# Decoder layer on one core: residual loads and row stores of the attentions move from the sync engine's queue to GpSimd's

## The reference

```
x = layernorm(x + causal_attention(x))            # 16 heads of 32, low-rank parts added to q, k, v, o weights
h = ln(x + attention(x, x)) ; h = ln(h + attention(h, ctx)) ; h = ln(h + relu(h @ fc1) @ fc2)
x = layernorm(x + h)
x = layernorm(x + bitlinear(gelu(bitlinear(x))))  # rows rounded to 8 bits, weights to -1, 0, 1
```

## Time and profile before

| | |
|---|---|
| median of 3 runs | 3247.62 us (3247.37 to 3250.29) |
| the profiled execution | 3245.53 us, span 3243.7 us |
| busy: PE, DVE, ACT, POOL | 2988.8, 2567.3, 1995.7, 1349.9 us |
| data moved by DMA | 405.86 MB, mean 125 GB/s |
| of it issued by SP (and a little by ACT) | 348.64 MB, 41.0% of the engines' time |
| issued by POOL | 51.40 MB, 5.1% |

### The profile page before, as it was taken

The page is one execution under the profiler, slowest core; times in us unless marked ns, Lnnn a source line. Parts: engine busy times, 40 slices in busy tenths (PEclk is TensorE's granted clock), DMA queues, the critical chain, the costliest instruction groups (busy, mean ns, idle before and its releaser), DMA issues.

```text
span 3243.7 us, 87025 instructions
## 1 busy us (share of the span) xinstructions
PE 2988.8 (92%) x34642; PEld 2369.2 (73%) x34642; DVE 2567.3 (79%) x4750; ACT 1995.7 (62%) x4650; POOL 1349.9 (42%) x1273
## 2 busy tenths in 40 slices
PE   7998999988999769999999999999889999999996
PEld 4987888888899647777877778877765565565662
DVE  4776888888899669999999999999846666666666
ACT  2655565667787537777777777877655445344352
POOL 0675632257765544444344344443132232222232
PEclk9999999999999889999999999999899999999997
DMA  4666655456554546655655555554341121211212
GB/s 127 185 206 223 194 180 153 135 159 202 174 162 140 150 118 134 141 141 125 140 137 134 137 135 147 134 129 106 125 152 40 46 53 53 56 45 44 56 40 49
DMA packets 430834, 405.86 MB, mean 125 GB/s; under 512 B 272368, under 2 KB 346240, under 8 KB 429280
## 3 DMA queue, kind: packets, MB, share of 16 engines
q1 hardware_dynamic: 415600, 348.64, 41.0%
q0 software_dynamic: 14576, 51.40, 5.1%
q10 hardware_dynamic: 256, 0.26, 0.0%
HBM read 239.98 MB, written 109.52 MB: 108 GB/s over the span
## 4 chain that ended last, share of the span: by engine, by line
PE 51%; DVE 18%; DMA 13%; ACT 8%; issue 4%; SPq 4%; POOL 1%; ACTq 0%; DVEq 0%; POOLq 0%
PE at_ps L769 22%; PE at_ps L1430 4%; PE at_ps L911 4%; PE at_ps L855 4%; DVE at_mx_cross L988 4%; DVE at_p L997 3%; DMA self_spill<-at_proj 3%; PE at_ps L1444 3%; PE at_ps L890 3%; PE at_ps L1455 3%; PE at_ps L1411 2%; ACT at_ps L945 2%; DVE at_proj L981 2%; DMA at_o_raw<-at_values 2%; PE at_ps L865 2%
## 5 line engine op out<-in xcount | busy, mean ns | idle before, releaser
L944 ACT ACTIVATE at_p<-at_ps 125x448 f16<-125x448 f32 (+2 forms) x1280 | 676.9, 529 | 285.9 <-PE at_ps L890 196.5
L997 DVE TENSOR_TENSOR at_p<-at_ps,at_p 125x448 f16<-125x448 f32 (+2 forms) x1280 | 750.5, 596 | 129.3 <-ACT at_ps L945 119.3
L945 ACT ACTIVATE at_ps<-at_ps 125x448 f32<-125x448 f32 (+2 forms) x1280 | 679.5, 531 | 0.0
L988 DVE TENSOR_REDUCE at_mx_cross<-at_ps 128x1 f32<-128x750 f32 x512 | 476.7, 931 | 26.9 <-PE at_ps L855 24.5
L1070 POOL TENSOR_TENSOR at_o_sum<-at_o_raw 128x256 f32<-128x256 f32 x192 | 121.2, 631 | 782.6 <-ACT at_o_raw L951 782.1
L911 PE MATMUL at_ps<-at_values,at_p 112*128 112x65 f16 (+3 forms) x6656 | 303.3, 185 | 23.4 <-DVE at_p L997 10.5
L1478 ACT ACTIVATE at_masks<-at_ps,at_b_cols 128x256 f32<-128x256 f32 x224 | 106.7, 476 | 336.2 <-PE at_ps L1411 336.1
L992 DVE TENSOR_REDUCE at_mx<-at_ps 112x2 f32<-112x448 f32 (+1 forms) x512 | 303.9, 609 | 10.0 <-PE at_ps L865 7.0
L1411 PE MATMUL at_ps<-at_xt,at_early 128*128 128x256 f16 x1792 | 302.1, 276 | 8.9 <-ACT at_w_first L1479 6.1
L911 PEld LDWEIGHTS at_ps<-at_values,at_p 112*128 112x128 f16 (+1 forms) x6656 | 267.2, 97 | 49.3 <-ACT at_o_raw L951 19.7
L1430 PE MATMUL at_ps<-at_w_second,at_w_first 128*128 128x512 f16 x896 | 283.6, 379 | 0.0
(11 more groups left out here) (217 smaller groups left out, 6941.7 us busy)
## 6 DMA issues: line engine op xcount, KB each, us to landing
at_x_res<-x SPq DMA_DIRECT2D x124, 256.0 KB, 3.2
cross_spill<-at_proj SPq DMA_DIRECT2D x64, 487.0 KB, 3.2
at_x_rows<-x SPq DMA_DIRECT2D x92, 256.0 KB, 3.1
at_prep<-bit POOLq DMA_DIRECT2D x32, 512.0 KB, 5.5
at_early<-ctx SPq DMA_DIRECT2D x32, 512.0 KB, 5.3
at_stacks<-cross_spill SPq DMA_DIRECT2D x64, 243.5 KB, 3.7
causal_spill<-at_proj SPq DMA_DIRECT2D x64, 224.0 KB, 3.5
at_stacks<-causal_spill SPq DMA_DIRECT2D x128, 112.0 KB, 2.3
```

The source lines that it names most:

```text
L944: act.activation(mem.p_hi[0:self.KC, n % 4, 0:self.P_COLS], scores, ACT.Exp, scale=EXP_SCALE)
L945: act.activation(scores, scores, ACT.Exp, scale=EXP_SCALE).then_inc(self.exp_done, 1)
L988: dve.tensor_reduce(self.mx[:, at, t, h:h + 1], mem.ps_qk[:, :, 0:self.KT // 2], AX.XY, ALU.max).then_inc(self.max_done, 1)
L997: dve.tensor_tensor(mem.p_lo[0:self.KC, n % 4, cols], mem.ps_st[0:self.KC, self.st_bank(b, g, n), cols], mem.p_hi[0:self.KC, n % 4, cols], ...
```

## The change

Events of kind `residual` and `store` do nothing on SP any more. POOL handles them, with the same semaphores, the same transfers, and at the same place of the list. In the feed-forward stage the first writing of `at_y` waits in addition until all stores of cross have landed.

```diff
--- before.py
+++ after.py
@@ -703,15 +703,6 @@
             to = mem.ct[b % 2].rearrange("p i c k -> p (i c) k")
             sp.dma_start(to[:, :, c * P:c * P + n_rows], mem.c_parts[0:n_rows, c].rearrange("p i d -> p (i d)"),
                          transpose=True).then_inc(self.ct_in[b % 2], 16)
-        elif kind == "residual":
-            if before is not None:
-                sp.wait_ge(self.stored, 32 * (b - self.NB + 1))
-            if b >= 2 and self.back(b, 2).has_wo:
-                sp.wait_ge(self.proj_free, self.free_index["y1", b - 2, 0] + 1)
-            elif b >= 2:
-                sp.wait_ge(self.z_done, b - 2 - self.NB + 1)
-            for t, q0 in enumerate(TILES):
-                sp.dma_start(mem.x_res[:, b % 2, t, :], self.x_in[b - self.b0, q0:q0 + P, :]).then_inc(self.x_res_in[b % 2], 16)
         elif kind == "spill":
             sp.wait_ge(self.proj_free, self.all_projected(b, g))
             wait(sp, self.stacked[g % 2], self.stack_count(b, g, 0))
@@ -729,13 +720,6 @@
         elif kind == "row":
             sp.wait_ge(*self.released(kind, b, g))
             sp.dma_start(self.qs(b, g)[96:97], self.mrow[:, g % 2, :]).then_inc(self.mrow_in[g % 2], 16)
-        elif kind == "store":
-            if self.norm is None:
-                sp.wait_ge(self.yn_done, 2 * b + 2)
-            else:
-                sp.wait_ge(self.y_done, b - self.NB + 1)
-            sp.dma_start(self.x_out[b - self.b0, 0:P, :], mem.y[:, 0, :]).then_inc(self.stored, 16)
-            sp.dma_start(self.x_out[b - self.b0, P:T, :], mem.y[2 * P - T:P, 1, :]).then_inc(self.stored, 16)
         elif kind == "weights in":
 
             for n in range(2):
@@ -1040,7 +1024,23 @@
 
     def gpsimd(self, pool, kind, b, g, n):
         mem, at = self.mem, b - self.b0
-        if kind == "split x":
+        if kind == "residual":
+            if self.before is not None:
+                pool.wait_ge(self.stored, 32 * (b - self.NB + 1))
+            if b >= 2 and self.back(b, 2).has_wo:
+                pool.wait_ge(self.proj_free, self.free_index["y1", b - 2, 0] + 1)
+            elif b >= 2:
+                pool.wait_ge(self.z_done, b - 2 - self.NB + 1)
+            for t, q0 in enumerate(TILES):
+                pool.dma_start(mem.x_res[:, b % 2, t, :], self.x_in[b - self.b0, q0:q0 + P, :]).then_inc(self.x_res_in[b % 2], 16)
+        elif kind == "store":
+            if self.norm is None:
+                pool.wait_ge(self.yn_done, 2 * b + 2)
+            else:
+                pool.wait_ge(self.y_done, b - self.NB + 1)
+            pool.dma_start(self.x_out[b - self.b0, 0:P, :], mem.y[:, 0, :]).then_inc(self.stored, 16)
+            pool.dma_start(self.x_out[b - self.b0, P:T, :], mem.y[2 * P - T:P, 1, :]).then_inc(self.stored, 16)
+        elif kind == "split x":
             pool.wait_ge(self.x_rows_in[b % 2], 32 * (b // 2 + 1))
             if at >= 1:
                 pool.wait_ge(self.xt_in[(b - 1) % 2], 32 * ((at - 1) // 2 + 1))
@@ -1618,6 +1618,8 @@
             self.row_stats(dve, self.z2, 2, self.y_dve, self.begun("y_dve", kind, b, tiles[0], 0), tiles)
         elif kind == "apply6":
             dve.wait_ge(self.y_pool, self.done("y_pool", "last", b, tiles[0]))
+            if b == 0:
+                dve.wait_ge(self.cross.stored, 32 * self.cross.b_end)
             wait(dve, self.stored, 32 * b)
             self.normalize(dve, self.y, self.z2, 2, tiles).then_inc(self.y_dve, 1)
```

## The result

The changed kernel took 3271.56 us in the median (3266.7 to 3277.53, 4 runs), the kernel before 3247.49 (3241.56 to 3250.29, 4 runs): ratio 1.0085, 95% interval 1.0068 to 1.0102. The change costs 24 us; 3232 was forecast. The profiled execution of the changed kernel took 3277.53 us, the highest of its four.

The account below looks back on a forecast made before the run. No engine was the whole bound: PE held half the span, a seventh hung on DMAs and the sync queue. Waits of 19.1 us times 0.8, plus 0.9 + 0.9, less 1.5, gave 15.6 us: 3232 us, range 3219 to 3249.

Parts of the forecast that it names:

- the seven waits behind a residual: Own layer: PE's stack waits after spills delayed by residual loads would all go, 9.7 us (bounds 4.9 to 9.7).
- eight waits behind store and load: Own layer: PE's stack waits after spills following stores and loads, 10.5 us in all; 4.5 us of gain taken.
- A wait costs its length: Own layer: a batch holding a 1.31 us wait and a short one took 28.0 us, one without waits 27.2.
- The stores: Moving them frees the sync queue: 4.5 us in own, 0.9 at the layer change, 0.9 ending cross, 1.0 lost in causal.
- The causal layer: Of its 5.5 us of PE waits for stacks, 2.0 would go, as the residual leaves between spill and stacks.
- POOL's price: Issuing on POOL takes 1.6 + 1.2 = 2.8 us a batch; delayed z costs DVE 1.5 us in all (0 to 16).
- The landings: Stores and residuals issued from POOL's queue would land in 3 to 4 us.
- The third rival: POOL's issues take twice as long, so z comes late and DVE loses 31 us: 3260 us, chance 0.13.
- The warning in the Trainium skill: Some DVE instructions lock the port through which GpSimd's DMA descriptors are written; SP or ACT advised; the rows showed no delay.
- The first rival: Shared 16 DMA engines set the landings, so spills stay late and only issue time is won: 5.8 us, 3242, chance 0.20.

Follow-up runs that it names:

- e2: The kernel before with only the stores moved to GpSimd, residual loads left on the sync engine: 3239.78 us, ratio 0.9958 to 0.9991.
- e4: The kernel before plus two small unread GpSimd loads at each place where the changed kernel issues a residual or store: 3243.07 us, ratio 0.9971 to 1.0008.
- e9: The changed kernel with residual loads cut to an eighth of their bytes from each layer's third batch on: 3243.85 us, ratio 0.9962 to 1.0004.
- e5: The kernel before, all on the sync engine, residual moved behind the stack loads in causal and own layers: 3246.53 us, ratio 0.9975 to 1.0022.
- e8: The kernel before with stores on GpSimd and, in the own layer, the sync engine's residual behind the stack loads: 3231.86 us, ratio 0.9937 to 0.9968.
- e1: The kernel before with only the residual loads moved to GpSimd, stores left on the sync engine: 3262.21 us, ratio 1.0030 to 1.0067.
- e11: The kernel before with residual loads on the scalar engine's queue and stores on GpSimd's: 3257.83 us, ratio 1.0001 to 1.0056.

## Why the prediction was wrong

**The step that failed** is the one on the seven waits behind a residual: "so that its data is through, or nearly, when the spill starts". I set the residual's new moment (901.8 + 1.2 us) against the *next* spill at 906.61 only. But the earlier trace rows already held the unit before: a spill at 898.59 that lands after 5.2 us, so with stack loads at about 904. At 903.0 the residual is a microsecond ahead of them. That step was booked at -9.7 us, and the other unit, whose loads it hits, at nothing. The seven waits behind the former residual (0.60 to 2.21 us) did go. In their place the unit before, where eight waits behind store and load had been 0.34 to 2.36 us, 10.5 in all, got seven of 2.30 to 4.50, 21.5 in all. The former residual's spill was not quicker either (4.73 us from 856.02 to its stack loads, 4.72 before), against the 2.8 that was reckoned with.

**The clock** was in no term. Between own's first and last z the idle time grew by 10.0 and 11.3 us in the two executions; PE's busy time by 13.4 and 7.7, at the lower granted clock. "A wait costs its length" was read from the one of 1.31 us, which held full clock; five of the longer ones of before already did not (24 matmuls took 3.40 us instead of 2.46 behind the wait of 2.36), and this was to be seen in the same trace.

**The stores** were right in sign, and roughly in size: booked at 4.5 in own, 0.9 at its end and 0.9 in cross, less 1.0 in causal and 1.5 for POOL, some 3 us with the factor of 0.8; alone they brought 7.0 (e2, by the interval 3 to 14). Of PE's waits for the self stacks e2 loses only 3.4 of 26.1 us, so the gain did not come by that step alone.

**The causal layer** was booked at -2.0 and lost 4.5 and 5.3 us in two executions. The text noted that "in the causal layer the residual goes out between spill and stacks" and took this for a harm to be removed. In one queue the spill went first; on POOL the residual runs ahead of it, and 14 spills take 1.4 us longer.

**POOL's price** held: a residual pair takes 1.08 us and a store pair 1.16 against 1.6 and 1.2 forecast, and DVE waits for z once in own, 3.3 us (0.7 before). The landings were said to be 3 to 4 us; in own they are 4.6 for the residual (3.3 before) and 2.6 and 4.1 for the two stores (2.3 and 3.0). The third rival gave the right sign, at 3260, for a reason that was not at work, as e4 shows. The warning in the Trainium skill that I cited with it (SBUF — State Buffer, "SBUF: two separate sides") is of descriptors written late, which issue times alone would not show. The 4 KB loads of e4 land after 3.0 us in own; no run has such loads on another queue, so the warning is neither seen nor excluded here.

**The first rival** had the right mechanism and the wrong place. It said that the same 16 engines serve both queues, and counted what is then not gained. That they also serve the stack loads, which the residual no longer stands behind, makes it a loss. The Trainium skill (DMA: Bandwidth & Descriptors, "Issuing engines are not separate DMA queues") says that transfers of all engines interleave on the same 16; e9 agrees as far as it goes, with 30 us for seven eighths of the bytes.

**What stays open:** why e5 does not gain where e8 does; what e1's loss is made of; why the two moves together cost more than their sum, in the changed kernel and in e11; why the causal layer loses up to 20 us in e11; what own's waits in e9 hang on. The addition of bytes to the kernel before, without moving anything, was not tried.

## What to carry to other kernels

A queue is also an order: here a transfer that was not urgent stood behind urgent loads in one queue, and moving it to another queue put it beside them. Before moving one, place its new moment against every transfer that the bottleneck waits for, the preceding unit's too, not only against the one it used to delay. Split such a change by kind of transfer: here one half brought 7 us and the other cost 15.5, and together they cost 24. On GpSimd the stores' issues shift the residual's moment, which may be a part of it; e11 shows that it is not all.

## What the runs showed of the hardware

Waits of PE for a DMA were followed by matmuls at 1.2 GHz for part of the next five microseconds behind six of seven waits of 2.30 to 4.50 us in the changed kernel, one of 3.10 being the exception, and behind five of 18 in the kernel before, the shortest of 1.83 us; over own the lower clock cost 13.4 and 7.7 us in two executions, the added idle time 10.0 and 11.3. Four issues more a batch on GpSimd's queue cost no measurable time. And with a 512 KB load issued 1.0 us ahead of a 224 KB spill on another queue, its stack loads went out 5.2 us behind the spill, while with the load issued 0.4 us behind it in the same queue they went out after 3.7 us.
